# First norm's x transposed by whole 128x128 products, second norm's deviation spread in column halves of 64: a shifted-window attention block in fp32

## The reference

```
xn = layernorm over channels(x) * g1 + b1
q, k, v = split(xn @ in_w.T + in_b)            # 8 heads of 8 channels
a = softmax(q k^T / sqrt(8)) v                 # within a window, per head
y = x + (a @ out_w.T + out_b) @ proj_w.T + proj_b
z = layernorm over channels(y) * g2 + b2
out = y + gelu(z @ fc1_w.T + fc1_b) @ fc2_w.T + fc2_b      # hidden 256
```

## Time and profile before

| | us |
|---|---|
| median of 3 runs (lowest to highest) | 87.61 (86.75 to 88.52) |
| profiled execution: its own time | 87.22 |
| its span, first to last instruction | 85.2 |
| outside the span | 2.0 |
| PE busy | 79.6 (93%) |
| DVE busy | 64.7 (76%) |
| ACT busy | 53.0 (62%) |
| POOL busy | 46.8 (55%) |

### The profile page before, as it was taken

One profiled execution on the slowest core, in us unless ns is written; L12 is line 12 of the kernel. 1 busy time (PEld: TensorE's weight loads), 2 busy tenths in 40 slices (PEclk: granted clock), 3 DMA queues, 4 the chain that ended last, 5 costly groups with the idle time before them and its releaser, 6 DMA issues.

```text
span 85.2 us, 4265 instructions
## 1 busy us (share of the span) xinstructions
PE 79.6 (93%) x1786; PEld 48.0 (56%) x1786; DVE 64.7 (76%) x208; ACT 53.0 (62%) x89; POOL 46.8 (55%) x58
## 2 busy tenths in 40 slices
PE   5999999889999999799999999999999999999950
PEld 5987757555865767467566637465464423533420
DVE  4999998969789989989789999997943944333260
ACT  0396798879888476588288356664587664725400
POOL 7988829989862972997634675787204041300000
PEclk9999999999999999999999999999999999999998
DMA  0799600121101122101021120000000000032042
GB/s 19 203 331 439 258 31 8 36 66 33 53 32 53 51 84 78 53 1 38 32 100 56 52 64 6 8 0 8 0 8 0 0 0 0 13 118 86 38 162 84
DMA packets 3490, 5.75 MB, mean 67 GB/s; under 512 B 944, under 2 KB 1712, under 8 KB 3344
## 3 DMA queue, kind: packets, MB, share of 16 engines
q1 hardware_dynamic: 2608, 3.08, 10.9%
q10 hardware_dynamic: 864, 2.40, 7.3%
HBM read 2.66 MB, written 1.05 MB: 44 GB/s over the span
## 4 chain that ended last, share of the span: by engine, by line
PE 65%; DVE 18%; issue 8%; DMA 3%; ACT 2%; SPq 1%; DVEq 0%; ACTq 0%
PE ps_s L333 14%; PE ps_u L426 6%; PE ps_u L499 5%; DVE row_max L656 4%; PE ps_m L307 4%; PE ps_s L483 4%; PE ps_t L333 3%; PE ps_t L483 3%; DMA masked<-qk 3%; PE ps_o L467 3%; PE ps_m L483 2%; PE ps_t L409 2%; PE ps_m L297 2%; PE ps_o L499 2%; PE ps_o L442 2%
## 5 line engine op out<-in xcount | busy, mean ns | idle before, releaser
L1058 POOL TENSOR_TENSOR max_x<-max_t,early 128x512 bf16<-128x512 bf16 x14 | 14.7, 1048 | 10.6 <-DVE max_t L669 10.6
L656 DVE TENSOR_REDUCE row_max<-ps_s 128x16 f32<-128x1024 f32 x15 | 18.1, 1209 | 2.5 <-PE ps_s L333 2.2
L915 ACT ACTIVATE probs<-ps_t 128x1024 f32<-128x1024 f32 x13 | 13.3, 1023 | 8.8 <-PE ps_t L409 8.4
L333 PE MATMUL ps_s<-masked,qk 32*64 32x256 f32 x240 | 16.9, 387 | 1.0 <-ACT probs L915 0.4
L333 PE MATMUL ps_t<-masked,qk 32*64 32x256 f32 x224 | 15.5, 387 | 0.0
L1067 POOL TENSOR_TENSOR rstd<-y_var,minus_half 128x4 f32<-128x4 f32 x8 | 8.1, 1010 | 9.9 <-DVE y_var L719 9.8
L333 PEld LDWEIGHTS ps_s<-masked,qk 32*64 32x64 f32 x240 | 8.1, 131 | 5.9 <-issue 2.9
L426 PE MATMUL ps_u<-probs,vz 128*32 128x64 f32 x512 | 10.5, 222 | 0.0
L426 PEld LDWEIGHTS ps_u<-probs,vz 128*32 128x32 f32 x512 | 7.9, 109 | 3.1 <-issue 2.7
L1043 POOL TENSOR_TENSOR rstd<-var,minus_half 128x4 f32<-128x4 f32 x8 | 8.3, 1043 | 1.0 <-DVE var L644 0.4
L282 PE MATMUL ps_t<-zeros 128*128 128x128 f32 x32 | 6.9, 376 | 1.0 <-DVE zeros L817 1.0
(11 more groups left out here) (111 smaller groups left out, 150.6 us busy)
## 6 DMA issues: line engine op xcount, KB each, us to landing
masked<-qk SPq DMA_DIRECT2D x38, 32.0 KB, 2.0
x_ch<-x_ch_d ACTq DMA_DIRECT2D x1, 1024.0 KB, 8.0
out_d<-result SPq DMA_DIRECT2D x3, 256.0 KB, 2.5
x_tok<-x_tok_d ACTq DMA_DIRECT2D x1, 512.0 KB, 6.0
masked<-qk SPq DMA_DIRECT2D x8, 64.0 KB, 2.4
late<-late_d ACTq DMA_DIRECT2D x1, 352.0 KB, 5.2
x_tok<-x_tok_d SPq DMA_DIRECT2D x2, 128.0 KB, 3.4
x_tok<-x_tok_d ACTq DMA_DIRECT2D x1, 256.0 KB, 4.8
```

Of the source, the lines that this page charges most:

```text
L333: return nc.tensor.matmul(ps[o:o + L, g, n * TOK:(n + 1) * TOK], qk[r:r + RG, b, w, t], masked[r:r + RG, b, :, w, t], start=(n == 0), stop ...
L656: nc.vector.tensor_reduce(row_max[:, w, 0:16], score_bank(k, w)[:].rearrange("q g (h j) -> q (g h) j", j=L), axis=AX.X, op=ALU.max).then_i ...
L915: nc.scalar.activation(probs[:, w, :], scores_t_bank(k, w)[:].rearrange("q g c -> q (g c)"), ACT.Exp).then_inc(probs_done, 1)
L1058: nc.gpsimd.tensor_tensor(max_x[:, k % 2, w, :].rearrange("q (n i) -> q n i", n=16), bf16_high(max_t[:, w, :]).unsqueeze(1).to_broadcast([ ...
```

## The change

Two edits on PE and one on ACT. `x_transpose` no longer issues, for each block of 128 columns, four 64x64 products on four parts of the array, but one `nc.tensor.transpose` of the whole 128x128 block: two calls per tile in place of eight. Its result stands in one PSUM bank (columns 0 to 255 of bank 0) in place of columns 0 to 127 of two banks, and in the order in which `xn` has it, so that `copy_xn` reads and writes plain rows of 256. `y_spread` of tiles 0 to 5 uses column groups of 64 (form 128*64, four calls) in place of 32 (form 128*32, eight calls), as tiles 6 and 7 did already. No wait and no order is changed.

```diff
@@ x_transpose(k)
                 for n in range(BLK):
-                    for u in range(2):
-                        r = slice(L * u, L * u + L)
-                        for w in range(2):
-                            c = n * P + C * w
-                            ins = nc.tensor.matmul(ps_m[C * w:C * w + C, u, n * L:(n + 1) * L],
-                                                   xhat[r, k % 2, c:c + C], ident[r, L * u:L * u + L],
-                                                   start=True, stop=True, tile_position=(L * u, C * w))
+                    ins = nc.tensor.transpose(ps_m[:, 0, n * P:(n + 1) * P],
+                                              xhat[:, k % 2, n * P:(n + 1) * P], ident)
                 ins.then_inc(x_transposed, 1)
@@ y_spread(k)
-                cols = 32 if k < TILES - 2 else C
+                cols = C
                 for b in range(BLK):
                     for c in range(0, P, cols):
@@ copy_xn(k)
-                nc.scalar.activation(xn[:, k % 2, :].rearrange("q (n u i) -> q u n i", n=BLK, u=2),
-                                     ps_m[:, :, 0:P].rearrange("q u (n i) -> q u n i", n=BLK),
-                                     ACT.Copy).then_inc(xn_copied, 1)
+                nc.scalar.activation(xn[:, k % 2, :], ps_m[:, 0, 0:TOK], ACT.Copy).then_inc(xn_copied, 1)
```

## The result

The kernel after takes 88.01 us (median of 11 runs, 87.88 to 89.9). The kernel before, run beside it, takes 87.88 (median of 11, 86.75 to 91.07). This one is 1.0096 with a 95% interval of 1.0049 to 1.0144: slower by 1.0%, about 0.8 us. The forecast was 1.8%: the direction and the range held, and the size is half. Note the floors: the quickest execution after is 87.88, the quickest before 86.75. After, nine of eleven executions lie within 0.4 us; before, they are spread over 2 us and more. That turned out to be the second half of the story.

The account below looks back on a forecast made before the run. The prediction took PE to bound most of the kernel, with DVE bounding some stretches. `y_spread` +1.26, `x_transpose` +0.35 and ACT's copy 0 gave +1.61 us on 87.22: 88.8 us, range 87.5 to 90.3.

Parts of the forecast that it names:

- What bounds the kernel, and the price of a change of form: PE mostly bounds the kernel, DVE some stretches; a group behind one of another array form pays about 0.15 us.
- the step back is free: Rival: the change from `y_spread`'s 128*64 to `y_sum`'s 128*32 costs nothing, or DVE's waits take more; 87.9 us, chance 0.15.
- The y term, +1.26: `y_spread` of tiles 0 to 5: no gain in own stream, added changes of form in slots 3 to 7 and tail, +1.26 us.
- Tile 5's +0.15: Tail: `y_spread` of tile 5 adds one change of form ahead of `y_sum`, all PE, +0.15 us.
- The x term, +0.35: `x_transpose`: the group takes 0.40 in place of 0.39 or 0.23; tiles 1, 3, 4, 5 and 7 counted, +0.35 us.
- The sum: Whole kernel: 1.26 + 0.35 = +1.61 us on the profiled 87.22, giving 88.8 us.
- forecast's own spread: Whole kernel: the main forecast, chance 0.52, with its own spread of 88.2 to 89.4 us.
- cheap case at 87.9: Whole kernel: `y_spread`'s sum falls from 1.26 to 0.36 us if 128*64 to 128*32 costs nothing; chance 0.15.
- Two records per transpose: Rival: `x_transpose` goes in two records a call, group 0.64 us, 1.2 to 1.4 more, 90.1 us; chance 0.20.
- Whole product at 0.21: Rival on `x_transpose`: its group falls to 0.21 us, 1.1 less over slots 1 to 3 and the start; chance 0.08.
- Clock: Rival: TensorE's granted clock falls to its lower level for some stretch, some 2 us more, 91 us; chance 0.05.
- not-slower rival: `x_transpose` group at 0.21 us: 87.7 us, or 86.9 to 87.2 if a third of `y_spread`'s changes is hidden; chance 0.08.

Follow-up runs that it names:

- y_only: Kernel before with only `y_spread` of tiles 0 to 5 changed to column groups of 64, the transpose left as before: 88.33 us, ratio to before 1.0118.
- x_only: Kernel before with only x transposed by whole 128x128 blocks, the spread left in quarters: 86.93 us in both groups of runs, ratio to before 0.9943 and 0.988.
- x_and_tile5: `x_only` with, of the spread, only tile 5 in column groups of 64: 87.02 us.
- x_only_more_calls: `x_only` with `project_out` as eight calls of 128 columns in place of four of 256: 88.19 us, ratio to before 1.0027.
- before_shift64: Kernel before with 16 one-column products added behind the first warm-up products, moving later PE records by 64: 94.20 us, ratio to before 1.0601.
- before_shift128: Kernel before with 32 one-column products added behind the first warm-up products, moving later PE records by 128: 97.56 us.

## Why the prediction was right, and where it was off

*What bounds the kernel, and the price of a change of form.* Right. 0.15 at each change was read from neighbours in the trace of before. After, the two new changes around `y_spread` cost 0.15 (0.44 to 0.59) and 0.13 (0.22 to 0.35), and `shift_scores` 0.12. The Trainium skill (TensorEngine Tiling, Key Properties) says that changing the tiling mode drains the engine. The trace agrees in so far as there is a price in both directions; that it is a drain can't be seen in it. The rival "the step back is free" is out.

*The y term, +1.26.* Nearly right: `y_only` costs 1.18% of its base, and after stands 1.08 us above `x_only`. By the chain, against `x_only`: slots 3 to 6 add 0.76 (58.19 less 57.34, less the 0.09 that the two are apart before slot 3), where 0.30 + 0.51 was forecast, and slot 7 adds 0.29, where it was 0.30 (its `y_sum` ends at 63.46 after and at 62.32 in `x_only`, 1.14 apart, less the 0.85). In the tail the distance stays 1.14. Tile 5's +0.15 was wrong: "all PE" overlooked that `y_sum(6)` waits for ACT's square, and `x_and_tile5` shows 0.

*The x term, +0.35.* This step failed. Its array part had the right sign and was too large: 0.37 for the group where 0.40 was taken, the changes of form as worked out, and in sum 0.15 by the chain at slot 3 (40.41 against 40.26), 0.1 between the quickest executions (86.81 against 86.75). But as measured against the kernel before as it typically runs, x gains 0.6% and 1.2%. It takes 224 instructions out of PE's stream, and no stall is left in the profiles of `x_only`; with 256 put back in another group, `x_only_more_calls` stalls twice and takes 88.19. The prediction priced calls by array time alone, and its sum took the profiled execution's 87.22 as a level, while 0.5 us of it was the stall at 41.53, which I had read as part of the batch. The group "one PE group after another with hardly a gap" had a gap inside it.

*The sum.* y's +1.0 (1.18%) and x's -0.5 (0.57%), each against the kernel before as it runs, leave +0.5 in place of +1.6; the ratio of the whole change gives +0.8, with an interval of 0.4 to 1.3, so the two parts add up within the measurement.

*What was luck.* The forecast's own spread was 88.2 to 89.4, and 88.01 lies below it. It falls into the part of the range that was there for the cheap case at 87.9, and the mechanism of that case, a free step back, is excluded.

*The other rivals.* Two records per transpose: excluded, one record a call. Whole product at 0.21: no, 0.37. The Trainium skill (TensorE: Matmul & The Clock Gate, Terms) has the transpose mode as "4× faster for FP32"; here, without the change of form ahead, the pair takes 0.22 as transposes and 0.49 as products, a factor of 2.2, and the measurement decides. Clock: granted 1.000 over the span of the kernel after, no effect of transposes seen. The not-slower rival was wrong in its mechanism, though its direction, that fewer calls help, was the right one for x alone. Its sum also counted 0.19 of saving on tile 3, where by the prediction's own account only 0.04 reached the end.

*A version that beats both.* `x_only`: 86.93 us in two groups of runs, ratio to before 0.994 and 0.988, and the tightest of all. The gain is small, and it lies in the long executions, not in the quickest. Take the transposes, leave the spread in quarters.

## What to carry to other kernels

Price a group of matmuls by its own stream plus 0.12 to 0.16 us for each neighbour of another array form, and put groups of one form side by side; a wider tile that halves the calls but stands alone between two others loses. On a PE that is nearly full, count instructions too (an fp32 product call was four, its transpose two): fewer of them went with fewer stalls of some half a microsecond that no semaphore explains. Before a sum is built on one profiled execution, look inside the batches for a piece longer than its siblings, and compare the floors of the runs as well as the medians.

## What was not expected of the hardware

PE stops inside a group, where the code has no wait, and the group takes 0.25 to 0.80 us longer; all ten such places in six profiles begin at a record 192 past a multiple of 256 of its stream, and at none of 164 such records does PE go on sooner than 1.27 us after the packet of instructions before it has landed. An fp32 transpose call of 128x128 is one weight load (138 to 143 ns) and one product record; the ordinary product of the same block is two and two, with loads of 186 to 192 ns. Products of one column on one and the same part of the array are not free, and have no fixed price: in `before_shift64` the records follow each other every 107 ns (32 in 3.5 us), in `before_shift128` every 58 ns for the first 57 and every 107 for the rest (64 in 4.3 us). In the first profile the warm-up products of the first 4.4 us likewise take 213 ns a record and those after 5.9 us mostly 111, while the granted clock reads 1.00 for both stretches; why was not tried.
